# Ternary feed-forward stage to linear attention: where the second attention's weights are split, its scale found and its first chunk loaded

## Time and profile before

| | us |
|---|---|
| median of 3 runs | 2650.17 (2649.89 to 2651.44) |
| the profiled execution's own time | 2649.13 |
| its span | 2647.1 |
| PE busy | 2425.0 (92%) |
| DVE busy | 1218.3 (46%) |
| ACT busy | 819.4 (31%) |
| POOL busy | 911.5 (34%) |

### The profile page before, as it was taken

How to read it: one execution, slowest core, us unless ns; L and a number is a source line. 1 busy time by engine, 2 the same in 40 slices (tenths; PEclk the granted TensorE clock), 3 DMA queues, 4 the chain that set the end, 5 groups by cost and what they waited for, 6 DMA issues and landing times. The chain is left out here.

```text
span 2647.1 us, 39886 instructions
## 1 busy us (share of the span) xinstructions
PE 2425.0 (92%) x12832; PEld 1797.7 (68%) x12832; DVE 1218.3 (46%) x2491; ACT 819.4 (31%) x1371; POOL 911.5 (34%) x1099
## 2 busy tenths in 40 slices
PE   7999699999999968599999994799999979999997
PEld 5888455555555436478888883588888858888886
DVE  3333477777777759611111112767677362111121
ACT  3222055555555531043344432111101112222221
POOL 0000156556556545233333332525153222222221
PEclk9999699999999988799999997899999989999999
DMA  6665735545544335400100103403212061000000
GB/s 246 226 226 191 175 91 126 120 117 122 126 117 117 80 109 190 147 17 32 48 32 32 32 16 111 148 33 126 95 63 95 9 202 49 32 32 32 32 33 32
DMA packets 154489, 255.29 MB, mean 96 GB/s; under 512 B 9648, under 2 KB 47536, under 8 KB 153904
## 3 DMA queue, kind: packets, MB, share of 16 engines
q1 hardware_dynamic: 137712, 208.20, 26.3%
q0 software_dynamic: 6144, 25.17, 2.9%
q10 hardware_dynamic: 10560, 20.97, 2.3%
HBM read 161.50 MB, written 92.27 MB: 96 GB/s over the span
## 5 line engine op out<-in xcount | busy, mean ns | idle before, releaser
L736 DVE CUSTOM_DVE_ANT_0 p_junk<-psum,p_causal 128x896 bf16<-128x896 f32 (+7 forms) x512 | 370.6, 752 | 159.2 <-PE psum L596 149.9
L699 ACT ACTIVATE p_probs<-psum 128x512 f32<-128x512 f32 (+1 forms) x640 | 331.3, 554 | 325.4 <-PE psum L607 319.9
L1130 POOL TENSOR_TENSOR p_h_lo<-p_h,p_h_hi 128x512 fp32r<-128x512 f32 x128 | 165.1, 1290 | 338.3 <-ACT p_h_hi L1159 338.3
L607 PE MATMUL psum<-p_qst,p_kst 98*128 98x512 f32 (+3 forms) x768 | 245.9, 384 | 17.3 <-ACT p_probs L699 10.9
L607 PEld LDWEIGHTS psum<-p_qst,p_kst 98*128 98x128 f32 x768 | 131.5, 190 | 170.3 <-ACT p_probs L699 84.8
L519 POOL TENSOR_SCALAR_AFFINE_SELECT p_probs<-p_probs 128x128 f32<-128x128 f32 x512 | 145.9, 305 | 263.8 <-ACT p_probs L699 263.0
L596 PE MATMUL psum<-p_kst,p_qst 96*128 96x512 f32 (+5 forms) x768 | 206.0, 369 | 20.5 <-DMA p_kst<-k_parts 17.0
L1762 POOL CAST p_h<-p_h 128x512 fp32r<-128x512 f16 x128 | 91.7, 716 | 372.9 <-ACT p_h L1786 372.9
L845 PE MATMUL psum<-p_xT_hi,tern 128*128 128x512 f32 x512 | 206.2, 403 | 1.4 <-DVE p_xT_lo L1224 1.4
L1195 PE MATMUL psum<-tern,p_h_hi 128*128 128x512 f32 x512 | 203.0, 397 | 2.2 <-POOL p_h_lo L1130 2.2
L845 PE MATMUL psum<-p_xT,p_w_hi 128*128 128x512 f32 x512 | 203.2, 397 | 0.7 <-ACT p_xT L1773 0.7
(11 more groups left out here) (174 smaller groups left out, 4764.2 us busy)
## 6 DMA issues: line engine op xcount, KB each, us to landing
p_qst<-q_parts SPq DMA_DIRECT2D x96, 256.0 KB, 4.6
p_kst<-k_parts SPq DMA_DIRECT2D x96, 256.0 KB, 6.9
q_parts<-p_qk_out SPq DMA_DIRECT2D x32, 512.0 KB, 2.8
k_parts<-p_qk_out SPq DMA_DIRECT2D x32, 512.0 KB, 2.8
ffn_x<-x SPq DMA_DIRECT2D x12, 1024.0 KB, 5.6
p_x<-in_x_t POOLq DMA_DIRECT2D x8, 1024.0 KB, 6.4
p_raw<-in_f_w POOLq DMA_DIRECT2D x8, 1024.0 KB, 7.9
v_rows<-p_v_out SPq DMA_DIRECT2D x32, 256.0 KB, 4.8
```

Of the source, the lines that this page charges most:

```text
L607: mm = pe.matmul(ST_BANKS[st % 2][:, col:col + CH - q0], kst[s][0:KD + 2, g, j * P:(j + 1) * P], qst[s][0:KD + 2, c, g, q0:CH], start=True ...
L699: act.activation(probs[:, n % 2, g, col:CH], ST_BANKS[st % 2][:, col:CH], ACT.Exp, scale=SM_SCALE).then_inc(p_ready, 1)
L736: dve.tensor_tensor_reduce(halves_of(junk[:, which, 0:n]), scores, halves_of(causal[:, SEQ - n:SEQ]), 1.0, FLOOR, ALU.add, ALU.max, rowmax ...
L1130: pool.tensor_tensor(h_lo[:, m % 2, :], h[:, m % 2, :], f32(h_hi[:, m % 2, :]), ALU.subtract).then_inc(hl_done, 1)
```

## The change

The change touches `phase_ffn0`, `phase_linear_attention` and `build_program`.

- Wq, Wk and Wv arrive as one array. In each of the first three batches of `phase_ffn0`, SP loads the two halves of one of them into `kept` (a buffer that the phase before used), ACT copies the `hi` part at step 4 of the chunk, and DVE subtracts the `lo` part ahead of its other work of that chunk. The results lie in buffers that both phases hold. Wo is still split in the linear attention.
- At the start of the last batch, SP loads y and x1 of chunk 0 into the buffers of the next phase.
- `ys` of the ternary stage is the second half of the next phase's `ys`. SP no longer waits for the last store at the end of `phase_ffn0`; it does so in the next phase, behind the load of Wo.
- DVE's eviction and maximum are interleaved (evict 0, evict 1, maximum 0, evict 2, ...).
- The maximum over the partitions is found by DVE (a copy that widens a column to 128), PE (a transpose) and DVE (a reduction), and the scale and its reciprocal are computed there, at the end of `phase_ffn0`. POOL's `partition_all_reduce` is gone.
- In the linear attention ACT does the first `part_hi` ahead of the split of Wo and the wait for the constants. POOL's split of Wo (two pieces) stands between its layer norm parts of chunk 0 and chunk 1. DVE waits for the split ahead of its loop.

```diff
 def phase_ffn0(...)
+        ys = after.ys[:, 1, :].rearrange("p (t d) -> p t d", t=CT)
+        w_stage = kept.rearrange("p n i k -> p n (i k)")
 # sync
                 def body(b, last):
+                    if not last:
+                        for c in range(2):
+                            sp.wait_ge(w_lo_done, 2 * b + c + 1)
+                            sp.dma_start(w_stage[:, c, :].rearrange("p (k n) -> p k n", n=D),
+                                         after.qkv_w[bass.ds(b, 1), 2 * c * P:(2 * c + 2) * P, :].rearrange("o (k p) n -> p (o k) n", p=P)
+                                         ).then_inc(w_loaded[c], 16)
                     load_x(b, 1)
                     if not last:
                         load_x(b + 1, 0)
+                    else:
+                        sp.wait_ge(y_stored, 1 + 32 * b)
+                        sp.dma_start(after.ys[:, 0, :]..., y_dram[0]...).then_inc(next_loaded, 16)
+                        sp.dma_start(after.x1[:, :]..., x1_dram[0]...).then_inc(next_loaded, 16)
-                sp.wait_ge(y_stored, 1 + 16 * NCH)
+                sp.wait_ge(next_loaded, 32)
 # scalar, in step t of chunk c, behind h_hi and x_hi
+                            if t == HT // 4 and not last:
+                                act.wait_ge(w_loaded[c], 16 * b + 16)
+                                act.activation(w_half(after.w_hi, b, c), w_stage[:, c, :], ACT.Copy).then_inc(w_hi_done, 1)
 # tensor, behind the loop
+                pe.wait_ge(run_max, NCH + 1)
+                pe.transpose(T.bank(0)[:, 0:P], max_cols[:, :], ident[:, :]).then_inc(max_turned, 1)
 # vector, at the head of each chunk
+                        if not last:
+                            dve.wait_ge(w_hi_done, 2 * b + c + 1)
+                            dve.tensor_tensor(w_half(after.w_lo, b, c), w_stage[:, c, :], f32(w_half(after.w_hi, b, c)),
+                                              ALU.subtract).then_inc(w_lo_done, 1)
 # vector, behind the loop
-                dve.tensor_copy(y_max[:, :], y_abs[:, CT + 1:CT + 2]).then_inc(run_max, 1)
+                dve.tensor_copy(max_cols[:, :], y_abs[:, CT + 1:CT + 2].to_broadcast([P, P])).then_inc(run_max, 1)
+                dve.wait_ge(max_turned, 1)
+                dve.tensor_reduce(quant[:, 0:1], T.bank(0)[:, 0:P], AX.X, ALU.max).then_inc(quant_step, 1)
+                dve.wait_ge(quant_step, 1)
+                dve.tensor_scalar(quant[:, 1:2], quant[:, 0:1], 1.0 / QMAX, FP4_EPS, ALU.mult, ALU.add).then_inc(quant_step, 1)
+                dve.wait_ge(quant_step, 2)
+                dve.reciprocal(quant[:, 2:3], quant[:, 1:2]).then_inc(quant_step, 1)

 def phase_linear_attention(...)
+        y_loaded = [sem("p5_y_loaded0", 16), sem("p5_y_loaded1")]
+        x1_loaded = sem("p5_x1_loaded", 16)
 # sync
-                load_y(sp, 0, 0)
-                load_x1(sp, 0, 0)
+                load_w(sp)
+                sp.wait_ge(y_stored, 1 + 16 * NCH)
                 load_y(sp, 0, 1)
-                load_w(sp)
 # gpsimd
-                pool.partition_all_reduce(quant[:, 0:1], y_max[:, :], P, bass.bass_isa.ReduceOp.max).then_inc(max_all, 1)
-                split_lo(pool, 0, 2)
                 ln_a.pool_part(pool, 0)
-                split_lo(pool, 2)
+                split_lo(pool)
                 ln_a.pool_part(pool, 1)
 # scalar
-                split_hi(act)
-                act.wait_ge(consts_loaded, 16 * 6)
                 part_hi(0, 0, a_x)
-                act.wait_ge(w_done, n_w)
+                split_hi(act)
+                act.wait_ge(consts_loaded, 16 * 6)
 # tensor
-                        pe.wait_ge(w_done, 2 * n + 2)
+                        if n == 3:
+                            pe.wait_ge(w_done, n_w)
 # vector
-                dve.wait_ge(max_all, 1)
-                dve.tensor_scalar(quant[:, 1:2], ...)
-                dve.reciprocal(quant[:, 2:3], ...)
                 dve.wait_ge(consts_loaded, 16 * 6)
+                dve.wait_ge(w_done, n_w)
```

More of the change, by code:

```diff
@@ L10 @@
 from contextlib import ExitStack
+from dataclasses import dataclass
 import numpy as np
@@ L1068, in _, with phase_ffn0 @@
                 dve.tensor_tensor(alpha[:, :], totals_all[:, 0:2], per_count[:, :], ALU.mult).then_inc(alpha_step, 1)
-def phase_ffn0(nc, psum, ident, tern, alpha, b1, b2, x1, x1_dram, y_dram, y_max):
+def phase_ffn0(nc, psum, ident, tern, kept, alpha, b1, b2, x1, x1_dram, y_dram, y_stored, after):
     with Phase(nc) as ctx:
@@ L1095, in phase_ffn0 @@
         passed = sem("p4_passed")
+        next_loaded = sem("p4_next_loaded")
         bias_loaded, x_loaded, cleared = sem("p4_bias_loaded"), sem("p4_x_loaded", 16), sem("p4_cleared")
@@ L1100, in phase_ffn0 @@
         y_done, y_maxed, run_max = sem("p4_y_done"), sem("p4_y_maxed"), sem("p4_run_max")
-        y_stored = sem("p4_y_stored", 1)
+        w_loaded = [sem(f"p4_w_loaded{c}") for c in range(2)]
+        w_hi_done, w_lo_done = sem("p4_w_hi_done"), sem("p4_w_lo_done", 2)
+        max_turned, quant_step = sem("p4_max_turned"), sem("p4_quant_step")
+        w_half = lambda ap, b, c: ap[:, bass.ds(b, 1), 2 * c:2 * c + 2, :].rearrange("p o k n -> p (o k n)")
         with nc.Block() as block:
@@ L1118, in body @@
                         load_x(b + 1, 0)
+                    else:
+                        sp.wait_ge(y_stored, 1 + 32 * b)
+                        sp.dma_start(after.ys[:, 0, :].rearrange("p (t d) -> p t d", t=CT),
+                                     y_dram[0].rearrange("(t p) d -> p t d", p=P)).then_inc(next_loaded, 16)
+                        sp.dma_start(after.x1[:, :].rearrange("p (t d) -> p t d", t=CT),
+                                     x1_dram[0].rearrange("(t p) d -> p t d", p=P)).then_inc(next_loaded, 16)
                     for c in range(2):
@@ L1234, in body @@
                         dve.wait_ge(y_stored, 1 + 32 * b + 16 * c)
[L1235 to L1243, removed]
+                        for a in range(CT + 1):
+                            if a < CT:
+                                m = CT * c + a
+                                Y.wait_full(dve, b, m)
+                                Y.free(dve.scalar_tensor_tensor(out=ys[:, a, :], in0=Y.bank(m), scalar=alpha[:, 1:2], in1=b2r[:, :],
+                                                                op0=ALU.mult, op1=ALU.add), m)
+                            if a > 0:
+                                Y.wait_freed(dve, a - 1, 2 * b + c + 1)
+                                dve.tensor_reduce(y_abs[:, a - 1:a], ys[:, a - 1, :], AX.X, ALU.max,
+                                                  apply_absolute_value=True).then_inc(y_maxed, 1)
                         dve.wait_ge(y_maxed, 8 * b + 4 * c + 4)
@@ L1247, in _, with phase_linear_attention @@
                 batches(dve, body)
-                dve.tensor_copy(y_max[:, :], y_abs[:, CT + 1:CT + 2]).then_inc(run_max, 1)
-def phase_linear_attention(nc, psum, ident, y_max, y_dram, x1_dram, wq, wk, wv, wo, bq, bk, bv, bo, decay_row, decay_col, residual, x3_dram, next_x3):
+                dve.tensor_copy(max_cols[:, :], y_abs[:, CT + 1:CT + 2].to_broadcast([P, P])).then_inc(run_max, 1)
+                quant = after.quant
+                dve.wait_ge(max_turned, 1)
[4 more added lines that the diff above has]
+                dve.reciprocal(quant[:, 2:3], quant[:, 1:2]).then_inc(quant_step, 1)
+@dataclass
+class Handover:
+    qkv_w: object
+    w_hi: object
+    w_lo: object
+    ys: object
+    x1: object
+    quant: object
+def phase_linear_attention(nc, psum, ident, got, y_dram, y_stored, x1_dram, wo, bq, bk, bv, bo, decay_row, decay_col, residual, x3_dram, next_x3):
     TT = SEQ // P
@@ L1263, in phase_linear_attention @@
         sem = ctx.semaphore
[L1264 to L1267, removed]
+        wo_hi = sb("p5_wo_hi", [P, KT, D], F32R)
+        wo_lo = sb("p5_wo_lo", [P, KT, D], F32R)
+        w_hi = [got.w_hi[:, n, :, :] for n in range(3)] + [wo_hi]
+        w_lo = [got.w_lo[:, n, :, :] for n in range(3)] + [wo_lo]
+        ys, x1, quant = got.ys, got.x1, got.quant
         x2 = sb("p5_x2", [P, TT, D], F32)
@@ L1286, in phase_linear_attention @@
         load_w, split_hi, split_lo, w_done, n_w = split_loader(
-            nc, ctx, "p5_w", qT[:, :, :], [job for n, w in enumerate((wq, wk, wv, wo)) for job in halves(w, w_hi[:, n, :, :], w_lo[:, n, :, :])])
+            nc, ctx, "p5_w", ks[:, :, :].rearrange("p (s k) n -> p s (k n)", s=4), halves(wo, wo_hi[:, :, :], wo_lo[:, :, :]))
         ln_a = LayerNorm(nc, ctx, "p5_ln_a")
@@ L1487, in product @@
                     def product(c, n, a_cols, w_cols, a_is_lhs):
-                        pe.wait_ge(w_done, 2 * n + 2)
+                        if n == 3:
+                            pe.wait_ge(w_done, n_w)
                         terms = []
                         for k in range(KT):
-                            for a, w in ((aT_hi, w_hi), (aT_lo, w_hi), (aT_hi, w_lo)):
```

(6 more changed lines are left out.)

25 lines of the change are left out of this document (10 added, 15 removed).

## The result

The changed kernel takes 2634.97 us (median of 6 runs, 2633.72 to 2635.65) against 2650.38 (6 runs) for the one before: ratio 0.9937, 95% interval 0.9927 to 0.9947. It is faster by 15.4 us where 23.5 were forecast, and its time lies outside the range. The profiled execution took 2634.95, its span is 2633.3.

What follows compares the result with a forecast made beforehand. PE was taken as the bound, idle some 53.7 us at the border before linear attention. Terms -14.4 - 3.2 - 8.1 - 2.0 + 4.0 + 0.2 = -23.5 took 2649.13 to 2625.6, median 2626.6; range 2621.5 to 2633 us.

Steps and rivals of the forecast that it cites:

- Tail and barrier: End of the ternary stage and border: earlier scale and no store wait start chunk 0's quantisation at 1624.45, not 1638.88: -14.4 us.
- Layer norm part: Chunk 0 of the linear attention: the wait for POOL's layer norm part falls from 4.78 to 1.58 us: -3.2.
- normalisation: Chunk 0 of the linear attention: with POOL silent beside it, normalisation falls from 10.04 to 1.92 us: -8.1.
- Transposes to first product: Chunk 0: without ACT's wait for constants, 7.28 us becomes 5.3: -2.0; PE's first products at half clock in both.
- Chunk 1: Linear attention: POOL's split of Wo takes turns with DVE's quantisation, +4.0 us; PE's second hole grows from 6.95 to about 11.
- Splits in the ternary stage: Ternary stage: six added ACT and DVE splits fit in idle time and cost 0, with a bound of 6 x 1.1 us.
- The ternary stage's head: Start of the ternary stage: 1 MB of weights queued behind the bias DMAs costs +0.2 us (0 to 1).
- From there on PE is nearly always fed, so whatever moves these products moves the end.: Linear attention after PE's second hole: a shift of the first products was taken to shift the kernel's end.
- the second's: Rival in the ternary stage: the added splits reach PE, each of six costing 1.1 to 1.2 us: 2633.5 us; chance 0.10.
- the third's: Rival at the linear attention's start: POOL's hidden wait of 8.46 us falls on its layer norm part: 2635 us; chance 0.06.
- the fourth: Rival in the ternary stage: late weight loads make the kernel slower than before, 2654.2 us at 24.4 us a load; chance 0.03.

Runs made afterwards that it cites:

- u1: The changed kernel with SP's wait for the last store of y put back at the end of the ternary stage: 2636.92 us.
- u2: The changed kernel with the scale found as in the kernel before, by POOL's reduction over partitions in the linear attention: 2651.68 us.
- f4: The changed kernel with Wo's two split subtractions on DVE behind chunk 1's normalisation, instead of on POOL beside its quantisation: 2630.84 us.
- f1: The changed kernel with 1376 bytes of padding ahead of the linear attention's own buffers: 2627.37 us.

## Why the prediction was wrong, point by point

- **Tail and barrier, -14.4.** Right: quantisation starts 14.6 us earlier. The new tail took 1.5 us as forecast (1622.16 to 1623.63), and the border 2.18 where I had 2.25. u1 and u2 show what it is made of: of the 14.6 us, the store's wait is worth 2.8 and the reduction 9.9 when each is put back alone; the other 1.9 were not separated.
- **Layer norm part, -3.2, and normalisation, -8.1.** Right by size (3.14 and 8.12). The account of the first had a gap: in the kernel before, POOL's hidden wait of 8.46 us stood ahead of the two `w_lo` that I blamed for the 4.78, and u2 shows that without those `w_lo`, but with the reduction, DVE waits 8.55 for POOL's part.
- **Transposes to first product, -2.0.** 7.28 fell to 4.95, so -2.3. What I said of the clock was wrong: the first 48 products ran at full clock (granted 1.00 from 1644 to 1656), while in the kernel before the granted clock was 0.57 from 1670 to 1674. PE had been idle for 15.81 us ahead of its transposes, instead of 46.46. The 48 products took 11.1 us instead of 12.3; the difference of 1.2 went into the second hole, which waits for DVE anyway.
- **Chunk 1, +4.0.** Right by size, 7.99 - 3.90 = 4.1, and in that DVE and POOL take turns (3.30 us for each of two instructions, 1.23 and 1.29 in f4); f4 takes 4.1 off. (Its working has a slip: it lets DVE's second instruction start at 2.9, before POOL's first ends at 3.1, and its last two figures, 7.4 against 3.6, differ by 3.8.) The hole became 12.3 rather than 11 because of the clock (the 1.2 us of the 48 products). Counted from the last ternary matmul, chunk 1's transposes came 24.0 us earlier; the terms up to there gave 23.7.
- **Splits in the ternary stage, 0.** Right: 486.7 us in both, and ACT is still idle for 1.35 us ahead of each gelu behind a split.
- **The ternary stage's head, +0.2.** It was 0: from the last operation of alpha (1111.43, 1112.98 in the changed kernel) to the first gelu are 13.5 us before and 13.4 after.
- **"From there on PE is nearly always fed, so whatever moves these products moves the end."** This is the step that failed. PE was fed, but 1152 matmuls with the handed-over weights took 0.2335 instead of 0.2267 us: 7.8 us. In f1, where the buffers that they meet lie 1376 bytes further on, 7.6 us come back by the medians and 7.6 in *border* and *rest*. I had priced every instruction that the change adds, moves or removes, and gave the sentence that the results "lie in buffers that both phases hold" no price.
- **The rivals.** The measured time is close to the second's and the third's, and neither happened: the ternary stage is as long as before (which also rules out the fourth), and POOL reached its layer norm part 0.2 us after the statistics. A time that fits a rival is no sign of it. The wait that the third rival named is real, however, and shows in u2, where the reduction was put back: POOL's part starts 7.1 us after the statistics.

## What to carry to other kernels

Where a change moves an operand of many matmuls, put the starts of both operands in the account: compare the distance of two matmul groups of one form before and after, since a step that is 3% longer (here 0.2333 us against 0.2267) shows in no wait of PE and in no busy share (7.00 of 7 us in both). It is worth looking at stages at 100% PE in this way too; here a pad of 1952 bytes gave 13.7 us. And a POOL reduction over partitions in a stage's head cost twice here (9.9 and 7 us in u2), once ahead of it and once ahead of the next ordinary POOL instruction that someone waits for.

## What the runs showed of the hardware that I had not expected

- The step of these float32r matmuls (128x128 by 128x512) depends on how far apart the starts of the stationary and the moving buffer are, modulo 256 bytes: 0.227 us when equal, 0.229 to 0.234 at the other distances tried (32, 64, 96 and 128, or 256 less those). At 64 it took two values in one execution, so the distance is not all that counts there. What makes the step longer was not settled, and the other distances were not tried.
- DVE's quantisation and POOL's subtraction take turns instruction by instruction: two instructions of 1.23 and 1.29 us took 3.30 each beside two POOL subtractions, and these took 6.48 together where two took 4.63 beside DVE's statistics.
- Behind the reduction over partitions POOL had a second hidden wait (8.46 us in the earlier trace rows), ahead of its next ordinary instruction. In u2 it was not over when that instruction's semaphore came, but 7.1 us later; without the reduction, in the changed kernel, the same instruction starts 0.2 us after the statistics. That the wait is served only then is my reading of this one gap.
